# Reordering one attention step and the beginning, and giving GpSimd the token scales of both feed-forward tiles

## What is computed

```python
x = x + tanh(g_xattn) * xattn(layernorm(x), ctx, ctx)     # softmax(q k^T / 4) v, then Wo
x = x + tanh(g_ffn) * ffn(layernorm(x))
# ffn:
h = bit_linear(x, w1)          # 256 -> 1024; act_quant per token (127 / max|x|), weights to -1, 0, 1
h = silu(depthwise_conv1d(h))  # 3 taps along the tokens, with a bias
return bit_linear(h, w2)       # 1024 -> 256
```

## Time and profile before

| | us |
|---|---|
| timed runs, median of 3 (284.3 to 286.65) | 286.36 |
| the profiled execution | 285.66 |
| its span, first to last instruction | 283.9 |
| mean granted TensorE clock, as a share of full speed | 0.964 |
| busy: PE / DVE / ACT / POOL | 219.6 / 200.8 / 148.1 / 133.8 |

### The profile page before, as it was taken

How to read it: one execution, slowest core, us unless ns; L and a number is a source line. 1 busy time by engine, 2 the same in 40 slices (tenths; PEclk the granted TensorE clock), 3 DMA queues, 4 the chain that set the end, 5 groups by cost and what they waited for, 6 DMA issues and landing times.

```text
span 283.9 us, 6533 instructions
## 1 busy us (share of the span) xinstructions
PE 219.6 (77%) x2408; PEld 177.7 (63%) x2424; DVE 200.8 (71%) x406; ACT 148.1 (52%) x264; POOL 133.8 (47%) x233
## 2 busy tenths in 40 slices
PE   0696779987988789889889899888756856764773
PEld 0675657766867678678768777766634644553663
DVE  0305134788687588988988988978569969998672
ACT  1040816445446366675675684674845446565350
POOL 3202020623623438568567676546485646554331
PEclk9997959999999999999999999999997979999799
DMA  6938110100101101001001000000000100110111
GB/s 206 320 79 268 37 28 11 38 22 21 38 4 38 29 12 39 18 21 39 20 21 25 29 9 2 0 3 2 0 1 2 37 18 21 37 37 22 37 39 57
DMA packets 11553, 11.97 MB, mean 42 GB/s; under 512 B 1026, under 2 KB 11266, under 8 KB 11522
## 3 DMA queue, kind: packets, MB, share of 16 engines
q1 hardware_dynamic: 11522, 11.55, 13.0%
HBM read 9.45 MB, written 2.10 MB: 41 GB/s over the span
## 4 chain that ended last, share of the span: by engine, by line
PE 42%; DVE 20%; issue 17%; ACT 9%; POOL 8%; DMA 1%; SPq 1%; POOLq 0%; DVEq 0%; ACTq 0%
DVE smax L782 9%; PE ps_proj L366 6%; PE ps_av L417 6%; PE ps_proj L358 5%; PE ps_score L393 5%; PE ps_score L374 4%; POOL hid L293 3%; DVE y L838 3%; PE ps_max L403 3%; ACT y L656 3%; PE ps_av L427 2%; PE ps_av L522 2%; POOL zdeq L305 2%; PE ps_av L570 2%; PE ps_h L470 2%
## 5 line engine op out<-in xcount | busy, mean ns | idle before, releaser
L782 DVE TENSOR_REDUCE smax<-ps_max 128x8 f32<-128x1024 f32 x32 | 39.1, 1222 | 25.4 <-PE ps_max L403 25.4
L630 ACT ACTIVATE prob<-ps_score 128x1024 f32<-128x1024 f32 x32 | 32.8, 1024 | 21.0 <-PE ps_score L393 20.5
L393 PE MATMUL ps_score<-Qs,KT 32*128 32x128 f32 x512 | 37.1, 282 | 4.2 <-DVE smax L782 2.3
L403 PE MATMUL ps_max<-KT,QT 32*128 32x256 f32 x256 | 36.3, 400 | 1.5 <-DVE smax L782 1.5
L393 PEld LDWEIGHTS ps_score<-Qs,KT 32*128 32x128 f32 x512 | 31.4, 186 | 9.3 <-issue 8.4
L270 POOL TENSOR_SCALAR var<-mv 128x1 f32<-128x1 f32 x16 | 3.9, 244 | 64.0 <-DVE mv L813 63.9
L838 DVE SCALAR_TENSOR_TENSOR y<-hid,conv,y 128x508 f32<-128x508 f32 x32 | 29.3, 915 | 6.2 <-ACT y L656 5.8
L656 ACT ACTIVATE y<-hid,conv 128x512 f32<-128x512 f32 x32 | 25.8, 814 | 14.6 <-DVE hid L831 9.4
L570 PE MATMUL ps_av<-w2q,zqT 128*128 128x256 f16 x128 | 18.7, 294 | 12.2 <-DVE xres L936 11.4
L841 DVE SCALAR_TENSOR_TENSOR y<-hid,conv,y 128x508 f32<-128x508 f32 x32 | 24.7, 773 | 1.1
L570 PEld LDWEIGHTS ps_av<-w2q,zqT 128*128 128x128 f16 x128 | 12.3, 105 | 19.9 <-DVE xres L936 17.3
(11 more groups left out here) (110 smaller groups left out, 543.3 us busy)
## 6 DMA issues: line engine op xcount, KB each, us to landing
xin<-x SPq DMA_DIRECT2D x16, 128.0 KB, 2.1
cin<-ctxT SPq DMA_DIRECT2D x16, 128.0 KB, 2.0
xres<-x SPq DMA_DIRECT2D x1, 2048.0 KB, 8.5
out<-xres SPq DMA_DIRECT2D x16, 128.0 KB, 1.7
w1f<-w1T SPq DMA_DIRECT2D x1, 1024.0 KB, 7.3
w2f<-w2T SPq DMA_DIRECT2D x1, 1024.0 KB, 9.1
wk<-wkT SPq DMA_DIRECT2D x1, 256.0 KB, 3.6
wv<-wvT SPq DMA_DIRECT2D x1, 256.0 KB, 3.9
```

Source lines behind the costliest of these rows:

```text
L393: mm = pe.matmul(ps_score[:, i * 512 + j * P:i * 512 + (j + 1) * P], KT[b % 3][rows, j * P:(j + 1) * P], Qs[rows, j * P:(j + 1) * P], star ...
L403: mm = pe.matmul(ps_max[:, i * 512 + t * 2 * P:i * 512 + (t + 1) * 2 * P], QT[n % 2][rows, t * P:(t + 1) * P], KT[n % 3][rows, t * 2 * P:( ...
L630: act.activation(prob[pair][:, :], ps_score[:, :], ACT.Exp, scale=DH ** -0.5).then_inc(exp_done, 1)
L782: dve.tensor_reduce(dst, ps_max[:, :].rearrange("p (g t e k) -> p g t e k", g=PG, t=KD, e=2), AX.X, ALU.max).then_inc(max_done, 1)
```

## The change

- **Beginning.** x is loaded once, a sequence at a time, into `xres`; `xin` and the 2 MB load are gone. The context has four buffers instead of two. The loads are reordered. The warm-up has 10 products and waits for `ident_done` only. VectorE makes the masks first and `ident16` later. `x_transpose(0)` moves behind `project_v(0)`, `x_copy(0)` behind `k_copy(0)`.
- **Weight sums** are four ACT passes of 1024 columns, two in step 0 and two in step 1; the means follow after step 1 instead of after step 0, the gate's tanh after step 0.
- **The step** of PE, ACT and DVE is reordered as the diff shows; `project_out` of a sequence comes one step later, into `ps_q` instead of `ps_av`; the taps of a step's tiles come in the next step.
- **Dequantisation.** Tiles 0 to 19 are all copied by ACT (two `raw` buffers) and multiplied by GpSimd; tiles 20 to 31 are all multiplied by VectorE out of PSUM.
- **The tail.** `quantise2(v)` waits until the taps of the tile of iteration v - 2's predecessor are done; `exponent(15, 1)` stands behind `middle_tap(18)`; `normalise(15)` stands ahead of `token_scale(0)`; a small Silu loads ACT's table early.

```diff
-WARM = 14
+WARM = 10
+CB = 4
...
+FIRST_LATE = 20
...
-        ps_o = ps_av[:, 0:D]
+        ps_o = ps_q
...
+        def on_gp(T):
+            return T < FIRST_LATE
+        def gp_tiles(T):
+            return min(T, FIRST_LATE)
+        def dve_tiles(T):
+            return T - gp_tiles(T)
...
             def load_x(i):
-                wait(sp, xn_done, i - 1)
-                sp.dma_start(xin[i % 2][:, :], x[i * P:(i + 1) * P, :]).then_inc(x_in[i % 2], 16)
+                sp.dma_start(xres[:, i * D:(i + 1) * D], x[i * P:(i + 1) * P, :]).then_inc(x_in[i], 16)
...
-            load_x(0)
             load_c(0)
             load_w(wk, wkT, KD, wk_in)
+            load_x(0)
             load_w(wv, wvT, KD, wv_in)
...
             def dequantise(T):
                 G = T // NC_
-                gp.wait_ge(raw_done, T // 2 + 1)
+                gp.wait_ge(raw_done, gp_tiles(T) + 1)
                 gp.wait_ge(xq_done, 2 * SB * (G + 1))
                 wait(gp, conv_done, T - HB + 1)
-                gp.tensor_tensor(hid[T % HB][:, :], raw[:, :], deq[:, G * GT:(G + 1) * GT],
-                                 ALU.mult).then_inc(even_done, 1)
+                gp.tensor_tensor(hid[T % HB][:, :], raw[T % 2][:, :], deq[:, G * GT:(G + 1) * GT],
+                                 ALU.mult).then_inc(scaled_gp, 1)
             def quantise2(v):
                 gp.wait_ge(zs_done, v + 1)
+                if v - 2 in LATE:
+                    gp.wait_ge(conv_done, LATE[v - 2][-1])
...
-                for T in TILES.get(s, ())[0:1]:
-                    dequantise(T)
                 if seq(s - 2):
                     round1(s - 2)
+                for T in TILES.get(s, ()):
+                    if on_gp(T):
+                        dequantise(T)
...
             def x_transpose(n):
                 pe.wait_ge(xn_done, n + 1)
                 wait(pe, q_done, n)
-                wait(pe, aT_done, n - 2)
+                wait(pe, x1_done, n - 2)
...
             def step(s):          # PE
-                if seq(b):
-                    max_transpose(b)
-                if seq(d - 1):
-                    int_transpose(d - 1, min(tiles, default=0))
-                if seq(n):
-                    project_v(n)
+                if seq(d):
+                    project_out(d)
                 if seq(a):
                     weigh(a)
                 if seq(n):
+                    x_transpose(n)
+                if seq(b):
+                    max_transpose(b)
+                if seq(a):
+                    unweighted_transpose(a)
+                if seq(n):
+                    project_v(n)
                     project_q(n)
+                if seq(d - 1):
+                    int_transpose(d - 1, min(tiles, default=0))
                 for T in tiles[0:1]:
                     hidden(T, s - 2)
-                if seq(a):
-                    unweighted_transpose(a)
                 row_stage(b, 0)
...
-                if seq(a):
-                    project_out(a)
-                if seq(n + 1):
-                    x_transpose(n + 1)
...
             pe.wait_ge(ident_done, 1)
-            pe.wait_ge(ident16_done, 1)
             for i in range(WARM):
                 pe.matmul(ps_av[:, 0:P], ident[:, :], ident[:, :], start=True, stop=True)
-            x_transpose(0)
...
             def step(s, extra=lambda k: None):          # ACT
+                last = TILES.get(s - 1, ())
                 if seq(a):
                     exponent(a, 1)
-                if seq(d - 1):
-                    int_copy(d - 1)
-                if seq(n):
-                    x_copy(n)
+                for T in last[0:1]:
+                    middle_tap(T)
+                extra(0)
                 if seq(a):
                     u_copy(a)
                 if seq(n):
+                    x_copy(n)
+                extra(1)
+                for T in last[1:2]:
+                    middle_tap(T)
+                if seq(n):
                     v_copy(n)
                     q_copy(n)
+                if seq(d - 1):
+                    int_copy(d - 1)
...
                 for T in tiles[0:1]:
                     raw_copy(T)
-                extra(0)
                 exponent(b, 0)
+                for T in tiles[1:2]:
+                    raw_copy(T)
                 if seq(a):
                     att_copy(a)
-                for T in tiles[0:1]:
-                    middle_tap(T)
                 if seq(n + 1):
                     k_copy(n + 1)
-                for T in tiles[1:2]:
-                    middle_tap(T)
-                extra(1)
...
+            middle_tap(18)
             exponent(NB - 1, 1)
+            act.activation(scratch[:, :], ones[:, 0:1], ACT.Silu)
+            act.wait_ge(w2q_done, PIECES)
             act.wait_ge(w1q_done, PIECES)
-            act.wait_ge(w2q_done, PIECES)
+            u_copy(NB - 1)
             silu(0)
             int_copy(NB - 3)
-            u_copy(NB - 1)
-            raw_copy(20)
+            middle_tap(19)
+            att_copy(NB - 1)
...
             def step(s, extra=lambda k: None):          # DVE
-                for T in before[-1:]:
+                for T in last[0:1]:
                     outer_taps(T)
+                if seq(a):
+                    normalise(a)
                 if seq(d):
                     quantise1(d)
-                if seq(a):
-                    normalise(a)
                 if seq(n):
                     row_max(n, 1)
-                for T in tiles[1:2]:
-                    dequantise(T)
+                for T in last[1:2]:
+                    outer_taps(T)
                 extra(0)
                 extra(1)
-                if s < NB - 1:
-                    for T in tiles[:-1]:
-                        outer_taps(T)
...
             residual1(NB - 2)
             outer_taps(18)
+            normalise(NB - 1)
             token_scale(0)
-            normalise(NB - 1)
+            dequantise(20)
+            outer_taps(19)
             quantise1(NB - 2)
-            outer_taps(19)
             residual1(NB - 1)
+            token_scale(1)
             dequantise(21)
-            token_scale(1)
             outer_taps(20)
             quantise1(NB - 1)
...
                 for T in LATE.get(v, ()):
                     outer_taps(T - 1)
-                    if T % 2:
-                        dequantise(T)
+                    dequantise(T)
```

More of the change, by code:

```diff
@@ L93, in build @@
         w_deq = sb("w_deq", [P, 2])
-        xin = [sb(f"xin{i}", [P, D]) for i in range(2)]
-        cin = [sb(f"cin{i}", [P, KD * P]) for i in range(2)]
+        cin = [sb(f"cin{i}", [P, KD * P]) for i in range(CB)]
         xres = sb("xres", [P, NB * D])
@@ L125, in build @@
         deq = sb("deq", [P, NB * P])
-        raw = sb("raw", [P, GT])
+        raw = [sb(f"raw{i}", [P, GT]) for i in range(2)]
+        scratch = sb("scratch", [P, 1])
         hid = [sb(f"hid{i}", [P, GT]) for i in range(HB)]
@@ L527, in _ @@
             project_v(0)
+            x_transpose(0)
             pe.wait_ge(wq_in, 16)
@@ L532, in _ @@
             row_stage(-1, 1)
-            x_transpose(1)
             pe.wait_ge(v_ones, 2)
@@ L572, in project_down @@
                 pe.matmul(ps_f, shift16[:, :], w2sum[:, :], start=False, stop=True).then_inc(f_ready, 1)
+            project_out(NB - 2)
+            weigh(NB - 1)
             int_transpose(NB - 3, 20)
-            weigh(NB - 1)
             hidden(20, NB - 2)
@@ L697, in _ @@
             k_copy(0)
+            x_copy(0)
             v_copy(0)
@@ L700, in _, with weight_sums, half @@
             k_copy(1)
-            def weight_sums(k):
-                if k == 0:
-                    act.wait_ge(w1_in, 16)
-                    act.activation(y[:, 0:KD * HID], w1f[:, :], ACT.Abs, accum_out=abs_sum[:, 0:1])
-                else:
-                    act.wait_ge(w2_in, 16)
-                    act.activation(y[:, KD * HID:2 * KD * HID], w2f[:, :], ACT.Abs,
-                                   accum_out=abs_sum[:, 1:2]).then_inc(abs_done, 1)
-            step(0, weight_sums)
-            act.wait_ge(mean_done, 1)
+            def weight_sums(first):
+                def half(k):
+                    i, w, loaded_w = ((0, w1f, w1_in), (1, w2f, w2_in))[first]
+                    act.wait_ge(loaded_w, 16)
+                    ac = act.activation(y[:, (2 * i + k) * HID:(2 * i + k + 1) * HID], w[:, k * HID:(k + 1) * HID], ACT.Abs,
+                                        accum_out=abs_sum[:, 2 * k + i:2 * k + i + 1])
+                    if first == 1 and k == 1:
+                        ac.then_inc(abs_done, 1)
+                return half
+            step(0, weight_sums(0))
+            act.wait_ge(gate_ready, 1)
             act.activation(gate[:, :], ps_setup[:, 0:2], ACT.Tanh).then_inc(gate_done, 1)
-            for s in range(1, SB + 2):
+            step(1, weight_sums(1))
+            for s in range(2, SB + 2):
                 step(s)
@@ L747, in _ @@
```

(16 more changed lines are left out.)

110 lines of the change are left out of this document (47 added, 63 removed).

## The result

| | before | changed |
|---|---|---|
| median | 286.24 us (284.3 to 287.25) | 282.85 us (281.04 to 284.11) |
| ratio | | 0.9875, 95% interval [0.9842, 0.9908] |
| span of the profiled execution | 283.9 | 280.8 |

The change makes the kernel some 1.2% faster, 3.4 us between the medians and 3.1 between the two spans. 279 was forecast, a gain of 6.2 against the profiled execution: the sign is right, the time lies in the range, and the size of the gain is half of what was promised.

A forecast was written before the change was run, and what follows sets the result against it. It saw no full engine in steps 7 to 14, an alternating chain, and VectorE bounding the tail loop. Terms -13.1 - 1.6 - 0.3 + 9.2 + 3.2 - 3.6 = -6.2 took 285.66 to 279.5, rounded to 279; range 264 to 284.

The forecast's parts named there:

- The collision in steps 7 to 14: Steps 7 to 14: conv taps and GpSimd's multiplications block each other in alternation, 12.0 a step, +9.2 us; chance 0.50.
- (b): Steps 7 to 14: the late tap gets in first, 10.85 a step, -0.2 instead of +9.2, total 270; chance 0.17.
- (c): Steps 7 to 14: taps and multiplications don't block each other, 10.5 a step, total 265.7; chance 0.20.
- The beginning: Steps 0 and 1: earlier, shorter warm-up, split weight sums and no clock fall in step 1, together -13.1 us.
- the cost of the moved x_copy(0): Beginning: x_copy(0) now stands behind the K copies, costing +0.7 us.
- the clock of step 0: Beginning: step 0's dip (0.83) kept as it is, while step 1's fall should not come, -2.1 us.
- (e): Beginning gives back only half, because TensorE stays at the lower clock or weights arrive late; total 285, chance 0.06.
- Steps 2 to 5: Steps 2 to 5: the reordered step saves 0.39 us each, -1.6 for four.
- step 6: Step 6: the same reordering gain, less a new wait ahead of hidden, -0.3 us.
- Step 15: Step 15 and start of the tail: later exponential, token_scale(0) and more VectorE work, +3.2 us.
- The tail loop: Tail loop: taps no longer collide, -5.3; five more VectorE multiplications, +3.0; shorter way in iteration 2, -1.3; sum -3.6 us.
- The rest: The last 19.33 us after the tail loop: no change.

The follow-up runs named there:

- e1: Changed kernel with GpSimd's two multiplications of a step replaced by two fills that read nothing, token scales left out; one execution at 277.22 us.
- e3: Changed kernel with the taps of the earlier step's second tile moved ahead of the second row maximum on VectorE; 275.75 us, ratio 0.9659.
- e9: Changed kernel with GpSimd's multiplications waiting until the previous step's conv taps are done, VectorE's order kept; 276.02 us, ratio 0.9643.
- e12: e11 with integer transposes and copies early in steps 7 to 15, and only the first late tap ahead of the second row maximum; 265.63 us, ratio 0.9238.
- e5: Changed kernel with a one-column ScalarE copy ahead of the first K copy's waits, so the table loads early; 281.07 us, ratio 0.9839.
- e6: e5 plus 5, 6 and 3 unread identity products in TensorE's three idle stretches of the beginning; 278.94 us, ratio 0.9762.
- e11: e3, e6 and e10 combined in one kernel; 271.11 us, ratio 0.944.
- e10: Changed kernel with the last exponential, exponent(NB - 1, 1), ahead of middle_tap(18) on ScalarE; 282.35 us, ratio 0.9852.
- e2: Changed kernel with the odd tile of each step multiplied by VectorE again, behind the second row maximum; 277.33 us, ratio 0.9698.
- e8: e3 with int_transpose moved right behind max_transpose on TensorE and int_copy right behind x_copy on ScalarE; 278.55 us, ratio 0.9727.
- e13: Changed kernel with only TensorE's idle stretches of the beginning filled (11, 6 and 3 products), table load left in place; one execution at 280.0 us.
- e14: The changed kernel unaltered, profiled once more; one execution at 280.93 us.
- e7: Changed kernel without GpSimd's wait for the conv taps ahead of quantise2 in the tail loop; 288.03 us, ratio 1.0091.
- e4: Kernel before, with the two 16-bit identity copies moved ahead of the first norms on VectorE; one execution at 278.92 us.

## Why the gain was half of the forecast

**The collision in steps 7 to 14** (+9.2, measured +8.2): right, in place, order and size. Who goes first, the taps of 1.65 and the period of 12.05 are as worked out from the earlier trace rows. A tap behind a running multiplication, which no row of before showed, behaves like the tap behind GpSimd's pass: it ends some 0.55 after the multiplication. One figure is right without a working: 10.43 and a multiplication of 1.27 make 11.70, not the 11.56 of the prediction. Measured, the second multiplication ends at 11.57, since it issues behind the first at 9.85 and takes 1.72 beside the tap. The 1.0 between the two lies mostly in the last of the eight steps, which took 11.13 (anchors 177.68 and 188.81).

**Rivals (b) and (c)**: both were priced from a floor that was too low. (c) said 10.5 a step without collisions; e1, e3 and e9 give 11.05. What failed in it is "TensorE's work, 10.0, its copy wait, and a short wait for the exponential": TensorE's work is 9.94 as said, but the copy wait is 0.95 when nothing covers it, not 0.75 less a cover by the anchor's slack, and the wait for the exponential adds 0.16. So the new order alone costs 0.17 a step against the 10.88 of the earlier trace rows; e12, which takes that wait away, gets 10.26.

**The beginning** (-13.1, measured -8.7) is the step of the prediction that failed, in two of its terms: the cost of the moved x_copy(0), and the clock of step 0.
- "Against that x_copy(0) now stands behind the K copies: +0.7" missed that the K copy is now ScalarE's first work, so that the table load stands behind its waits and on the path. In before it ran at once, under the loads. Predicted anchor 0: 15.2; measured 16.9. From TensorE's first product behind the warm-up to anchor 0 it is 8.60 in before and 10.84 here, so the term measures +2.2. e5 took 1.28 out of TensorE's wait, and in e6, with the clock at 1.00 as well, the same stretch is 9.27: +0.7, as said.
- "Without the idle time the fall should not come: -2.1. I keep step 0's dip (0.83) as it is" was half the thought. It did not come in step 1 (10.61 at clock 1.00, against 11.55 at 0.74 in the earlier trace rows). But the kernel before already had idle stretches of 0.67, 1.53 and 1.05 between its warm-up and its first max_transpose, and with them the dip of 0.83:

```profile
19.13 1.13 PE L351 MATMUL ps_proj<-cin,wk 128*128 128x128 f32 x8 [0.67 <-ACT V L619]
...
22.85 1.13 PE L403 MATMUL ps_max<-KT,QT 32*128 32x256 f32 x8 [1.53 <-DVE smax L782]
...
25.40 1.00 PE L374 MATMUL ps_score<-ident,smax 128*128 128x128 f32 x4 [1.05 <-DVE smax L782]
```

  In the changed kernel they are 2.62, 1.53 and 0.78, so the one ahead of block 0's Q is 2 longer, and the fall in step 0 became larger: 11.96 at 0.57 where some 9.4 had been expected. With 1.34 in place of the 2.62 (e5) step 0 is 10.16 at 0.83, with all three filled 8.51 at 1.00. A dip was treated as the property of a step; it belongs to what TensorE did before it.

With both causes gone, anchor 2 stands at 34.12, 35.27 and 34.84 (e6, e11, e12), where the prediction had 35.1: the rest of that sum holds within 1. That the median of e6, 278.94, falls on the 279 of the forecast is luck: its profiled execution took 277.22, with steps 7 to 14 at +8.1, step 15 at +4.1 and the last stage at -1.4.

Rival (e) had named this loss, with a chance of 0.06: the beginning gives back only part, since TensorE stays at the lower clock. The beginning gave back two thirds of what was forecast, where (e) has half (and half of 13.1 makes 286, not its 285). The other reason that it gave, late weights, is not needed: in e6, e11 and e12 the weights arrive by the same transfers, and the sum holds.

**Steps 2 to 5, step 6**: right within 0.3.

**Step 15** (+3.2, measured +2.9): right in sum, in part by luck. weigh(15) came at 10.98 after the anchor instead of 11.65, normalise(15) at 16.39 instead of 17.35, and yet the stage is only 0.3 shorter than forecast: some 0.7 was lost behind it. Its mean clock is 0.89 against 0.96 in before, 0.69 to 0.89 over the runs of the new order, and at 0.79 the stage is 31.9 (+4.1): the clock was not in the sum. e10 shows that 0.9 of the loss is the exponential's place.

**The tail loop** (-3.6, measured -2.3): right, but for the clock. The taps are 0.74 again, and 3.95 lies between most residual2's, as predicted. One iteration takes 5.06, since VectorE waits 1.02 for `hidden`. In the changed kernel and in e6, that iteration:

```profile
235.56:240.62 5.06, 5.06 (x38) 4.24 (x36) 3.94 (x8) 2.91 (x4) 1.41 (x2) 0.68 0.07 26
```
```profile
231.35:235.30 3.95, 2.91 (x30) 2.31 (x29) 3.85 (x8) 2.43 (x4) 1.40 (x2) 1.00 0.09 33
```

TensorE fills the whole iteration at a mean clock of 0.68, and has 2.91 of work in it at 1.00. The loop took 42.2 in nine other runs (e1, e2, e3, e5, e6, e8, e9, e10, e13), which is -3.4 against the earlier trace rows, 43.3 in the three where this iteration took 5.06 (the changed kernel, e12, e14), and 42.7 in e11, where it took 4.40. The Trainium skill (SBUF — State Buffer, Who interferes with whom) says that the order of issue decides who blocks. The trace agrees in e7 as in the earlier trace rows: the second to issue waits. In e7 the tap of 1.43 is held for 0.69 of the 0.90 that it overlaps the pass.

**The rest** (0, measured -1.3): the work is the same; 19.33 at a clock of 0.92 in the earlier trace rows, 18.88 at 0.94 in e7, 17.93 to 18.01 at 0.97 and 0.98 (the changed kernel, e3, e6), and up to 19.66 at 0.91 in e11. The clock again, with the other sign: this 1.3 is no gain of the change.

## What to carry over

Two operations that block each other cost time only on the engine that sets the end. Where they overlap with a small lead (0.16 here, either way), ask which of the two has room, and give it the wait: e9 does so with one line and gains 2.4%. Before a stall is said to go, list the idle stretches that stay or grow elsewhere, since TensorE's clock followed them in all fourteen executions of this beginning; and what becomes ScalarE's first work also pays for its table load. Try the largest term of a change alone: here three moved lines brought 7 us (e4).

## What was not expected of the hardware

- The granted clock of the beginning varies between executions of one program: step 0 at 0.57 (11.96 us) and at 0.74 (10.48 us, e14) for the changed kernel, always 1.00 and 8.51 when the waits left to TensorE ahead of block 0's Q and of the first max_transpose were 0.22 and 0.29 (e6, e11; 8.52 in e12).
- ScalarE's table load of 1.28 stands right ahead of its first operation and behind the waits that stand there, so it starts only when they are fulfilled (8.38), though ScalarE had been idle from 0. With a small operation ahead of the waits (e5, e6) it starts at 0.72.
- A GpSimd fill, which reads nothing, beside the late taps left them at 0.74 and 0.75 (e1); the multiplication, which reads two operands, made them 1.65.
- A held operation does not lose the whole overlap: a late tap of step 10 overlaps the multiplication by 1.11 and is 0.92 longer, the tap of e7 by 0.90 and is 0.69 longer.
